# Linear attention in a 25-step decoder: key features before query features, key-value products beside the query features

## What is computed

```python
q, k, v = x @ w_qkv.T                       # 128 channels each, 16 heads of 8
phi(a)  = elu(a @ proj) + 1                 # 32 features a head, 512 in all
kv      = sum over tokens of phi(k) (x) [v, 1]      # per head 32 x 9
o       = phi(q) @ kv                       # per head 9 columns: 8 of values, 1 of the sum
attn    = o[:8] / (o[8] + 1e-8)
x       = layernorm(x + attn @ w_out + b_out) ...
```

## Time and profile before

| | |
|---|---|
| median of the timed runs | 4033.43 us (4032.87 to 4034.89) |
| the profiled execution, its device time | 4022.97 us |
| span of that execution in the trace | 4020.9 us |
| mean granted TensorE clock over the span | 0.974 of full |
| busy: TensorE matmul / VectorE / ScalarE / GpSimd | 93% / 68% / 49% / 25% |

### The profile page before, as it was taken

One profiled execution on the slowest core, in us unless ns is written; L12 is line 12 of the kernel. 1 busy time (PEld: TensorE's weight loads), 2 busy tenths in 40 slices (PEclk: granted clock), 3 DMA queues, 4 the chain that ended last, 5 costly groups with the idle time before them and its releaser, 6 DMA issues.

```text
span 4020.9 us, 70135 instructions
## 1 busy us (share of the span) xinstructions
PE 3726.8 (93%) x22966; PEld 2310.7 (57%) x22966; DVE 2715.9 (68%) x8004; ACT 1980.8 (49%) x5746; POOL 1014.8 (25%) x1109
## 2 busy tenths in 40 slices
PE   6999899999999998999988998999999999999997
PEld 4645446666565664566656444555656556646664
DVE  3787767676777745675457886777767777467663
ACT  1733345555555542575428214456555565317653
POOL 0154433222323301101110562322322232010012
PEclk8999999999999999999989999999999999999998
DMA  2100000001000002010210000000000100100101
GB/s 74 48 18 1 1 24 18 25 1 42 1 18 24 2 27 81 1 70 16 62 60 7 12 1 18 7 18 25 18 25 3 40 1 4 75 30 2 64 16 51
DMA packets 37011, 103.89 MB, mean 26 GB/s; under 512 B 3504, under 2 KB 28592, under 8 KB 33200
## 3 DMA queue, kind: packets, MB, share of 16 engines
q1 hardware_dynamic: 34608, 95.20, 6.7%
q0 software_dynamic: 2048, 4.20, 0.3%
HBM read 90.35 MB, written 9.04 MB: 25 GB/s over the span
## 4 chain that ended last, share of the span: by engine, by line
PE 71%; DVE 15%; ACT 6%; issue 5%; POOL 2%; DMA 0%; DVEq 0%; POOLq 0%; ACTq 0%; SPq 0%
PE ps_O L651 13%; PE ps_P L633 9%; PE ps_S L602 7%; PE ps_OUT L797 4%; PE ps_O L633 4%; PE ps_OUT L602 3%; ACT EX L734 3%; PE ps_P L1379 2%; PE ps_P L1671 2%; PE ps_S L1379 2%; PE ps_P L613 2%; PE ps_P L382 2%; PE ps_T L602 1%; PE ps_O L382 1%; PE ps_OUT L1162 1%
## 5 line engine op out<-in xcount | busy, mean ns | idle before, releaser
L651 PE MATMUL ps_O<-wide,V 128*64 128x256 f32 (+4 forms) x5152 | 596.8, 394 | 1.8 <-ACT wide L679 1.8
L734 ACT ACTIVATE EX<-NB,neg 128x154 f32<-128x154 f32 (+3 forms) x768 | 395.6, 521 | 114.3 <-DVE neg L762 114.3
L697 POOL COPY RX<-recips 128x256 f32<-128x256 f32 (+2 forms) x356 | 156.6, 440 | 1112.3 <-DVE recips L777 1102.8
L602 PE MATMUL ps_S<-KT,QT 64*128 64x154 f32 (+7 forms) x1936 | 375.0, 457 | 60.7 <-POOL QT L1684 25.4
L788 DVE TENSOR_TENSOR QT<-ps_O,RS 128x512 f32<-128x512 f32 x212 | 146.5, 691 | 383.2 <-PE ps_O L651 382.5
L681 DVE COPY wide<-ps_P 128x512 f32<-128x512 f32 (+4 forms) x528 | 339.4, 646 | 80.0 <-PE ps_P L633 77.9
L651 PEld LDWEIGHTS ps_O<-wide,V 128*64 128x64 f32 (+4 forms) x5152 | 267.0, 127 | 195.0 <-issue 111.3
L602 PE MATMUL ps_T<-KT,QT 64*128 64x154 f32 (+5 forms) x968 | 323.8, 437 | 6.0 <-ACT EX L734 3.2
L602 PE MATMUL ps_OUT<-KT,QT 64*128 64x154 f32 (+5 forms) x968 | 326.9, 437 | 0.1
L734 ACT ACTIVATE QT<-NB,neg 128x512 f32<-128x512 f32 (+2 forms) x512 | 318.6, 632 | 0.0
L633 PE MATMUL ps_P<-consts,EX 128*128 128x128 f32 (+1 forms) x1916 | 290.2, 287 | 25.0 <-ACT RS L688 11.7
(11 more groups left out here) (516 smaller groups left out, 8118.4 us busy)
## 6 DMA issues: line engine op xcount, KB each, us to landing
weights<-in_w_dram SPq DMA_DIRECT2D x10, 1664.0 KB, 6.9
weights<-in_w_dram SPq DMA_DIRECT2D x2, 6148.0 KB, 17.2
weights<-in_w5next_dram SPq DMA_DIRECT2D x6, 1664.0 KB, 7.0
weights<-in_w_dram SPq DMA_DIRECT2D x2, 4200.0 KB, 13.5
weights<-in_reltab_dram SPq DMA_DIRECT2D x2, 4096.0 KB, 13.3
weights<-in_w_dram SPq DMA_DIRECT2D x8, 640.0 KB, 3.7
weights<-in_w_dram SPq DMA_DIRECT2D x2, 2050.0 KB, 8.6
weights<-in_w_dram SPq DMA_DIRECT2D x2, 2048.0 KB, 8.1
```

The source lines that it names most:

```text
L602: ins = pe.matmul(S4[k][:, a * N:(a + 1) * N], QT[strip, c, qts[a] * P:(qts[a] + 1) * P], self.keys(c)[strip, 0:N], start=True, stop=True)
L651: ins = pe.matmul(O1[self.slot * j:self.slot * (j + 1), q0 * P:(q0 + self.nq) * P], self.value(c * self.hpc + j, kc), self.probs(rd, j)[:, ...
L697: pool.tensor_copy(RX[:, q0 * P:(q0 + self.nq) * P].rearrange("p (n s) -> p n s", s=self.slot), of.unsqueeze(2).broadcast_to([P, self.nq * ...
L734: ins = act.activation(ex[:, a * N:(a + 1) * N], src, ACT.Exp, bias=neg[:, at:at + 1], scale=-1.0 if self.added else 1.0, accum_out=sums[: ...
```

## The change

The loop of features takes the keys as chunks 0 to 3 and the queries as chunks 4 to 7, on TensorE, and through `feature` on VectorE and ScalarE. The KV products stand directly behind the eighth projection in TensorE's queue. The filler that stood ahead of them, and the wait for all eight chunks, stand behind them; the second filler, which stood behind `pe_head`, is gone from there. So there are as many fillers ahead of the query products as follows: before, one ahead of the KV products and one behind `pe_head`; after, one between the KV products and `pe_head`. Nothing else changes.

```diff
             def feature(self, c):
-                return self.qf[:, c, :] if c < 4 else self.kf[:, c - 4, :]
+                return self.kf[:, c, :] if c < 4 else self.qf[:, c - 4, :]
...
                     if c >= 4:
                         pe.wait_ge(r.ready, c - 3)
                     if c < 4:
-                        ins = pe.matmul(RING[c % 4][:, :], w("proj")[:, c * P:(c + 1) * P], self.qT, start=True, stop=True)
+                        ins = pe.matmul(RING[c % 4][:, :], self.kT[:, c * P:(c + 1) * P], w("proj"), start=True, stop=True)
                     else:
-                        t = c - 4
-                        ins = pe.matmul(RING[c % 4][:, :], self.kT[:, t * P:(t + 1) * P], w("proj"), start=True, stop=True)
+                        q = w("proj")[:, (c - 4) * P:(c - 3) * P]
+                        ins = pe.matmul(RING[c % 4][:, :], q, self.qT, start=True, stop=True)
                     ins.then_inc(r.hid, 1)
-                idle(pe, S[0])
-                pe.wait_ge(r.ready, 8)
                 pe.wait_ge(r.ones, 1)
                 for c in range(4):
                     for t in range(NT):
                         ins = pe.matmul(TB[:, c * 36:(c + 1) * 36], self.kf[:, t, c * P:(c + 1) * P],
                                         self.vv[:, t, 4 * c:4 * c + 4, :], start=(t == 0), stop=(t == NT - 1))
                 ins.then_inc(r.part, 1)
+                idle(pe, S[0])
+                pe.wait_ge(r.ready, 8)
                 self.nxt.pe_head(pe)
-                idle(pe, S[0])
                 pe.wait_ge(r.part_used, 1)
```

## The result

The changed kernel took 3995.0 us (median of four runs, 3989.6 to 3995.97), before 4033.15 in the same runs: ratio 0.9904, interval 0.9887 to 0.9922. Repeated in five rounds on another occasion it was 4001.72 against 4032.59, ratio 0.9919, interval 0.9906 to 0.9932.

What follows compares the result with a forecast made beforehand. The chain through TensorE, working by turns with VectorE in the features, was taken as the bound. A step of 4.28 - 3.41 + 2.59 + 5.29 = 8.75 us, 35.0 against 52.93, saves 17.9: 4015.5 us, range 4006.9 to 4023.4.

Steps and rivals of the forecast that it cites:

- the 3.41 us: Ahead of the KV products: they can start where the filler started, 3.41 us earlier a step, beside the last VectorE operations.
- the contention taken as 0: Weight loads beside VectorE's feature operations: could lose 0.09 us a step, taken as 0.
- Reordering the loop costs nothing.: Feature loop with keys first: same projections, same VectorE and ScalarE operations and operands, so no added time.
- I take the middle of 3.71 and 4.86, 4.28: KV products: 4.28 us a step, between the fastest 3.71 and 4.86, the mean of three of today's steps.
- For the query products I keep the mean of today, 5.29.: Query products: 5.29 us a step, from 21.15 / 4, with 3.71 and 6.69 as ends.
- `pe_head` and filler at 2.59: Between KV and query products: `pe_head` and one filler stay as before, 2.59 us a step.
- a term left as it was: Behind the query products: two fillers cover VectorE's normalisation, left as it is.
- 2.9 to 4.1 us: Sign in the profile after: first query product comes this long after the last L1123 ends, instead of some 7.4.
- The sum: Four changed steps: 8.75 us each from the filler's old start, 35.0 against 52.93, saving 17.9 us.
- high clock throughout: Rival: KV and query products at 3.71 each, 5.48 us a step, 31.0 saved, 4002.4 us; chance 0.08.
- slower: Rival: clock lost in 36-column products stays low in dense products behind, 37.4 us lost, 4052.9 us; chance 0.04.
- The range: Whole kernel: 4006.9 to 4023.4 us, from the forecast's own ends for KV and query products.

Runs made afterwards that it cites:

- run with four fillers: Kernel before with four fillers instead of one ahead of the wait for all eight chunks, no new order or overlap; 4013.82 us, ratio 0.9963.
- the doubled group: Changed kernel with the KV products made twice, 32 products instead of 16 a step; 4029.55 us, ratio 0.9993.

## Why the prediction was wrong

The direction and the mechanism of the first part, the earlier start, were right. What failed is the price of the clock: the terms for the KV products, for `pe_head` with its filler, and for the query products above all were taken from a profile in which the clock fell in the first of the groups or ahead of it, and the change moves that fall behind the first group, in two of the four steps behind both.

- *Where the chain runs, and the 3.41 us.* Right. The KV products started directly behind the eighth projection in all four steps, VectorE ended beside them, and its operations stayed at 677 to 692 ns, so the contention taken as 0 was 0 within 2 ns of the median. The wait for all eight chunks ended nothing.
- *"Reordering the loop costs nothing."* Right within 0.15% (interval 0.05 to 0.25%) by the run with the order alone, whose four steps were not longer.
- *"I take the middle of 3.71 and 4.86, 4.28" for the KV products.* This failed. They took 3.49 in each of the four steps. It is 3.2 us over the four. The argument took the clock's fall in the profile before, two values of it, as if it had to come at that distance again. And the price for the high clock, 3.71, came from a group that began at the low one (step 2 before, from 94.75), as this row of the profile before shows; at 2.4 GHz throughout, both groups take 3.49.

```profile
95.00:96.00 1.00, 1.00 (x10) 1.00 (x10) 0.00 (x0) 0.00 (x0) 0.00 (x0) 0.90 0.00 0
```

- *"For the query products I keep the mean of today, 5.29."* This failed more. They took 3.49, 3.49, 3.91 and 3.92, mean 3.70, 6.3 us less over the four. The argument looked at the KV products' cover alone and kept the clock of the second group, although the first group's new place changes what goes before the second. This is the largest of the misses.
- *`pe_head` and filler at 2.59.* This failed too: 2.59 is a price at the low clock, taken as fixed. They took 1.37, 1.38, 2.63 and 2.62: 2.4 us less in sum. Some 1.1 us more came behind the query products, in the fillers, a term left as it was. The four misses together are 12.9 us, which with 0.1 in the projections is, but for rounding, the whole way from the 17.9 forecast to the 31.0 measured. For the same reason the sign "2.9 to 4.1 us" from the last L1123 to the first query product was missed: it was 1.5 in step 1.
- *The sum.* 8.75 a step was forecast from the filler's old start; 36.78 less 13.64 is 23.1 over the four, 5.8 a step. The rival "high clock throughout" had 5.48 a step, 31.0 us saved and 4002.4 us, with a chance of 0.08. The four steps lost 31.0, and the second set of rounds gave 4001.7. That it agrees so closely is partly luck. Counted as the rival counts, without the 1.1 behind the query products, the saving is 29.8; its 3.71 for each group is too high, and in steps 3 and 4 the clock did fall between the groups. The evidence against it, a clock that fell behind query products near 98.6, is not wrong: in steps 1 and 2 of the changed kernel it fell behind them too, where it costs the groups nothing.
- *The rival "slower".* It was said to decide the sign once more than 26 of its 37.4 came true. The forecast saving is 17.9, so the sign turns at 17.9; 26 is that plus the 8 us that a measurement can tell. In the first profile after, the output projection is at its 1.16 in all four steps.
- *The range* reached only to the forecast's own ends. The rival lay at 4002.4, and the first median at 3995.0 was below that too, since the rest of the program varies by some 10 us. The text named that variation and gave it no width.

How the 31.0 us split: 13.8 is the earlier start (first feature projection to first KV product, 47.6 to 33.8). The other 17.2 is clock: KV products 7.4 (21.4 to 14.0), query products 6.3, what stands between them 2.4, and 1.1 behind. The run with four fillers shows that most of this part (16.1) can be had without the overlap. The run with the wait put back shows that the gap ahead costs both parts. No run had the overlap with a low clock in the KV products, so the 13.8 is read from starts and was not isolated by a run of its own.

What is open: why the kernel before varies from 4019 to 4045 us between executions. The two profiles of it put the difference outside the changed steps. The record says one thing more: over the 57 executions of it that the later runs were compared with, the time goes with the mean granted clock, from 0.979 at 4019.2 us to 0.971 at 4044.8 (correlation -0.95). The two profiled ones do not show it, though: 0.974 both, at spans of 4020.9 and 4036.1. No run here took it apart. Open too is why the clock falls between the groups in some steps and not in others of the same kernel.

## What to carry to other kernels

Price a sparse group of products by what stands ahead of it in TensorE's queue: moved from behind a wait to directly behind dense products, it ran in 3.5 us instead of 4.7 to 6.9. With the group behind it, and what lies between, the clock gave 17.2 us over four steps, more than the 13.8 of the earlier start. Where such a group must wait, fillers up to the wait's end gave 15 us here, and taking 0.9 us of dense products out between two such groups cost more than it saved. When a forecast hangs on the clock, give the case of all groups at the high level a real share, and widen the range by the spread of the rest of the program.

## What the runs showed that was not expected

The clock can fall while TensorE is busy without a gap: 0.56 from 49 to 50 in the doubled group. One filler of 0.9 us decided over 2 us of the next group (5.68 against 3.49). And the same queue up to the query products can go either way: with `pe_head` behind them they took 3.49 to 3.55 in all four steps of one profiled execution and 6.69 in three of four steps of the other, though the two kernels differ only in what stands behind.
